# The second batch's gathers moved behind the last quarter's modulation, and the third tile's maxima put ahead of the third quarter's combination

## The reference, cut to what matters

```
x  = x + gb * (w0 * y[expert0] + w1 * y[expert1])          # end of layer 0
h  = layernorm(x) * (1 + ca) + sa                          # 'modulation'
B  = (h W_qk) W_anchor^T * scale      # 16 heads x 64 anchors = 1024 logits a token
attn = softmax(B) over the 64 anchors of each head
s    = sum over tokens of attn
out  = attn ((attn^T v) / s)
x  = x + ga * (out W_out + b_out)
h  = layernorm(x) * (1 + cb) + sb
x  = x + gb * ffn(h)                                       # gated, three more layers
```

## Time and profile before

| | us |
|---|---|
| median of 3 runs | 779.26 (777.74 to 782.41) |
| the profiled execution | 780.26, span 778.5 |
| TensorE busy | 654.1 (84%) |
| VectorE busy | 570.3 (73%) |
| ScalarE busy | 400.4 (51%) |
| GpSimd busy | 277.6 (36%) |
| batch 0's attention up to its last sum | from about 301 to 363 |
| the same stage of batch 1 | up to 477 |
| mean granted TensorE clock | 0.926 |

### The profile page before, as it was taken

How to read it: one execution, slowest core, us unless ns; L and a number is a source line. 1 busy time by engine, 2 the same in 40 slices (tenths; PEclk the granted TensorE clock), 3 DMA queues, 4 the chain that set the end, 5 groups by cost and what they waited for, 6 DMA issues and landing times.

```text
span 778.5 us, 9648 instructions
## 1 busy us (share of the span) xinstructions
PE 654.1 (84%) x2985; PEld 470.0 (60%) x2985; DVE 570.3 (73%) x1441; ACT 400.4 (51%) x698; POOL 277.6 (36%) x229
## 2 busy tenths in 40 slices
PE   5777550399999995879989899899899899899897
PEld 2666540388878883446468555478555478556575
DVE  4889959279866736996976786866796866783763
ACT  3646233277777732334375444485443585442573
POOL 6457778200000026686202375211485120341100
PEclk9979755699999985989999999999999999999999
DMA  6441587778898610001000000000100000000000
GB/s 212 136 177 52 202 296 275 233 250 267 250 304 307 215 58 27 18 21 28 0 1 0 35 28 21 1 0 1 41 23 20 0 1 1 27 1 1 0 1 28
DMA packets 25779, 69.26 MB, mean 89 GB/s; under 512 B 5296, under 2 KB 8384, under 8 KB 24384
## 3 DMA queue, kind: packets, MB, share of 16 engines
q1 hardware_dynamic: 21632, 60.24, 23.0%
q0 software_dynamic: 4096, 8.40, 3.6%
HBM read 46.46 MB, written 22.16 MB: 88 GB/s over the span
## 4 chain that ended last, share of the span: by engine, by line
PE 58%; DVE 21%; POOL 7%; issue 6%; DMA 4%; ACT 4%; SPq 1%; DVEq 0%; ACTq 0%; POOLq 0%
PE ps L1685 14%; PE ps L1687 8%; PE ps L1681 8%; PE ps L1942 6%; PE ps L1689 6%; PE ps L1688 6%; DVE stats L1061 3%; POOL rows_by_expert L605 3%; PE ps L1960 2%; PE ps L1930 2%; DMA wbuf<-w_split 2%; DVE ring L1565 2%; DMA raw<-in_w 1%; DVE yb L1465 1%; DVE cmat L1641 1%
## 5 line engine op out<-in xcount | busy, mean ns | idle before, releaser
L652 POOL DMA_INDIRECT yb<-y_by_expert,ypos x64 | 63.3, 989 | 158.2 <-DMA y_by_expert<-ysb 142.6
L1685 PE MATMUL ps<-hid,fh 128*128 128x512 f32 x256 | 103.5, 404 | 5.1 <-DVE hid L1549 5.1
L1687 PE MATMUL ps<-hid,fh 128*128 128x512 f32 x256 | 101.4, 396 | 0.0
L605 POOL DMA_INDIRECT rows_by_expert<-h,pos x64 | 71.1, 1112 | 25.0 <-issue 18.9
L700 POOL TENSOR_TENSOR misc<-misc,ring 128x1024 f32<-128x1024 f32 x28 | 66.0, 2357 | 33.8 <-DVE ring L1539 28.7
L1549 DVE TENSOR_TENSOR hid<-ring,hid 128x512 fp32r<-128x512 f32 x56 | 38.6, 689 | 41.7 <-ACT hid L941 40.1
L1942 PE MATMUL ps<-ring,hn 128*128 128x512 f32 x112 | 56.5, 628 | 5.3 <-DVE ring L1539 5.3
L1685 PEld LDWEIGHTS ps<-hid,fh 128*128 128x128 f32 x256 | 48.2, 188 | 21.0 <-DVE hid L1549 10.3
L1960 PE MATMUL ps<-attnT,cmat 128*128 128x512 f32 x128 | 56.9, 592 | 0.0
L1687 PEld LDWEIGHTS ps<-hid,fh 128*128 128x128 f32 x256 | 48.3, 188 | 10.7
L998 ACT ACTIVATE ring<-ps 128x1024 f32<-128x1024 f32 x32 | 32.8, 1025 | 42.6 <-PE ps L1930 42.4
(11 more groups left out here) (326 smaller groups left out, 1702.4 us busy)
## 6 DMA issues: line engine op xcount, KB each, us to landing
wbuf<-w_split SPq DMA_DIRECT2D x46, 512.0 KB, 5.6
w_split<-parts SPq DMA_DIRECT2D x4, 2048.0 KB, 7.7
raw<-in_w SPq DMA_DIRECT2D x8, 512.0 KB, 8.5
xs<-rows_by_expert SPq DMA_DIRECT2D x16, 256.0 KB, 5.4
y_by_expert<-ysb SPq DMA_DIRECT2D x16, 256.0 KB, 4.5
ffn_raw<-in_ffn SPq DMA_DIRECT2D x1, 2816.0 KB, 11.1
rows_by_expert<-zeros SPq DMA_DIRECT2D x9, 256.0 KB, 2.5
xa<-in_x SPq DMA_DIRECT2D x4, 512.0 KB, 4.9
```

Of the source, the lines that this page charges most:

```text
L605: gp.indirect_dma_start(disp, bass.IndirectOffsetOnAxis(pos[:, b, k, t:t + 1].bitcast(U32), 0), h1[:, b % 2, t, :], None).then_inc(scatter ...
L652: gp.indirect_dma_start(yb[:, k, t, :], None, ydisp, bass.IndirectOffsetOnAxis(ypos[:, b, k, t:t + 1].bitcast(U32), 0))\
L1685: te.matmul(out_, w(0), x(0), start=first, stop=False)
L1687: return te.matmul(out_, w(0), x(1), start=False, stop=last_)
```

## The change

GpSimd's list in batch 0 loses the two gathers ahead of the first addition and those behind the additions of tiles 1 and 2. Three gathers now stand behind each of the additions of tiles 3 to 7, and the last one behind them; all 16 are still issued in batch 0. Later batches are as before. In VectorE's list `neg_max(2, 0)` comes ahead of `combine(0, 2)`.

```diff
                 if b == 0:
                     gather(0, places[14:16])
                     prepared(2, 0)
-                if more:
+                if b and more:
                     gather(b + 1, places[0:2])
                 for t in range(1, T):
                     pool.wait_ge(*dve_attn.now(t, b))
...
                     if b == 0 and t == 2:
                         modulate(3, 0)
-                    if more and t < T - 2:
+                    if b == 0 and t > 2:
+
+                        gather(1, places[3 * (t - 3):3 * (t - 2)])
+                    if b and more and t < T - 2:
                         gather(b + 1, places[2 * t:2 * t + 2])
                 if more:
-                    gather(b + 1, places[2 * (T - 2):])
+                    gather(b + 1, places[2 * (T - 2) if b else 3 * (T - 3):])
...
                 sums(0, b)
-                if b == 0:
-                    combine(0, 2)
                 if b:
                     residual("F", 1, ffn_bank(1, "y"), b - 1)
                 neg_max(2, b)
                 if b == 0:
+                    combine(0, 2)
                     normalized("L1a", 2, 0)
```

## The result

| | before | changed |
|---|---|---|
| median of 5 runs | 778.51 us (776.27 to 782.41) | 782.98 us (781.77 to 783.75) |
| ratio to before | | 1.0053, 95% interval 1.0027 to 1.0079 |
| profiled execution | 780.26, span 778.5 | 783.75, span 782.0 |
| mean granted clock | 0.926 | 0.927 |

The change made the kernel 4.5 us slower by the medians, 2.1 to 6.2 us by the interval. The forecast was 784.0, the range 778.0 to 788.0.

The account below looks back on a forecast made before the run. The chain of waits was taken to run through GpSimd's second addition and fourth-quarter modulation, then TensorE. Profiled 780.3 + 3.8 (late last sum) + 0.9 (clock) = 785.0 us, so median 784.0; range 778.0 to 788.0.

Parts of the forecast that it names:

- the two terms: First attention's end: TensorE's wait for GpSimd's last sum, +3.8 us, and its clock falling behind that wait, +0.9 us.
- rival (d): TensorE's clock falls long at 367, or again in the 6.2 us cycles: +7 to +8, 786.8 us; chance 0.15.
- Step 1: VectorE, third tile's maxima ahead of the third quarter's combination: root wait of 0.84 us exposed, second scaling about 1.0 us later.
- Steps 2 and 3: GpSimd's first two additions without gathers ahead: VectorE's fourth and fifth maxima casts held, third addition at 338.0 instead of 340.7.
- Step 4: Three gathers per tile on GpSimd: cycle 6.2 us, seventh addition at 364.65 instead of 360.50, TensorE's small matmuls +3.8 us.
- Rival (a): Gathers beside VectorE's scaling not stretched: cycle about 6.0, last sum 2.0 to 2.8 late, 781.7 us; chance 0.20.
- Step 5: TensorE's clock falls behind the wait for the last sum: +0.9 us after 0.85 slack, bounds 0 and +4.
- Rival (c): TensorE's gap at 329.7 closes, clock stays up, modulation earlier, attention ends 2.0 us earlier: 777.3 us; chance 0.08.

Follow-up runs that it names:

- e1: Kernel before with only the third tile's maxima moved ahead of the third quarter's combination, gathers as before; stage 73.01 us against 71.93, ratio 0.9983.
- e11: e6 with three gathers ahead of the fourth quarter's root and two between it and the second addition; stage 70.45 us, no ratio given.
- e8: Kernel before with three of its last four gathers moved between the sixth and seventh additions; stage 78.19 us, ratio 1.0067.
- e3: Changed kernel without gathers between the sixth and seventh additions, seven behind the last; stage 72.56 us, ratio 1.0027.
- e9: Kernel before with two of its last four gathers moved between the sixth and seventh additions; stage 76.99 us, ratio 1.0054.
- e10: e6 with VectorE's list of the kernel before; stage 68.12 us, no ratio given.
- e12: The kernel of e10 on a second occasion, timed against the kernel before; stage 68.12 us, ratio 0.9971.
- e6: Changed kernel with four gathers ahead of the fourth quarter's root, two behind additions of tiles 3 to 5, six behind the last; stage 68.66 us, ratio 0.9959.
- e5: e3 with one gather moved between the fourth quarter's root and the second addition; stage 72.70 us, no ratio given.
- e7: e6 with one more gather between the fourth quarter's root and the second addition, five behind the last; stage 70.48 us, ratio 0.9961.
- e2: Changed kernel with VectorE's old list, so only the gathers moved; stage 78.06 us, ratio 1.0052.
- e4: Changed kernel with three surplus 512-column matmuls on TensorE ahead of its first-batch wait for the last sum; stage 76.64 us, ratio 1.0028.

## Why the prediction was right

The path was the forecast one: the gathers make the last sum late, TensorE waits for it, and its clock falls behind the wait. The size was in part luck: +4.7 us forecast, +4.5 measured by the medians, with an interval of 2.1 to 6.2. By the stage, which repeats better, the two terms were off in opposite directions: 3.1 for the late last sum instead of 3.8, and 3.2 for the clock instead of 0.9, together 6.3 (6.36 at the outputs, 0.1 of it given back behind them). That lies between the forecast and rival (d), which had +7 to +8 for a long fall of the clock.

- **Step 1** said the second tile's scaling 1.0 later and the root's wait 0.84 exposed. Measured: 0.84, and the scaling ended 1.1 later (319.20 + 1.24 from t0, 9.81, against 320.73 + 1.26, 8.75). e1 confirmed +1.08 for the stage when this is done alone.
- **Steps 2 and 3** said additions at 323.1 and 332.0, casts held 1.2 and 2.0, the gap of TensorE 3.6, the third addition 338.0. On before's scale (+2.61) they came at 323.12 and 331.92, 1.28 and 1.96, 3.34, and 337.79. e11 showed that freeing the held cast with gathers brings nothing. The prediction did not say why the third addition comes earlier; the rows above do: the scaling of 3.27 us is back at 1.25.
- **Step 4** said the third gather is stretched and the cycles 7.1, 6.4 and 6.3, then 6.85; measured 7.06, 6.12, 6.11 and 6.80. The stretch was 0.1 us in the steady cycles. The step itself worked out a cycle of 6.2 and then wrote 6.4 and 6.3 without a reason; it was 0.7 us late by the sixth addition. e8 proved the last link by itself, e3 its reverse.
- **Rival (a)**: that the gathers are not stretched beside a scaling is refuted by 1.91, 1.76 and 1.08 us for gathers that start inside one. Its cycle of 6.0 was still nearer to the measured 6.12 than the forecast's 6.4, since the stretch is small where the scaling is nearly over. The inference of the Trainium skill that the prediction cites ("SBUF — State Buffer", section "Who interferes with whom"), by which a gather and a two-input scaling don't meet, does not hold for these gathers. Their rows name `ypos` as an input besides; whether what waits is the reading of it or the writing of the descriptors, no run separates.
- **Step 5** named the fall of the clock and mis-sized it. It lasted 6 us of full work, not 3, and the slack of 0.85 that I set against it was no cover: the slow products feed VectorE's `cmat` matrices, so VectorE's combinations behind them came 6.3 us later, as late as TensorE. I had misread: they show the end of four transposes and VectorE's next addition to x, which it reaches without idling; that interval is still 0.76 us in the changed kernel. The small matmuls took 1.7 us more, the products and what hangs on them 1.5. I had this as the upper bound (+4) and in rival (d), and should have taken what lay nearest, the fall at 332.5. Read rightly, that row also gives the size: a mean of 0.67 over 9.8 us, the rest at 1.0, is 6.5 us at half clock, an estimate of 3.2 us lost and not 4.
- **When the clock falls** could not be worked out from a few rows of one execution. It fell behind the last sum as forecast. But it also fell behind 1.60 us in e9, and did not fall behind 2.03 (e1), 2.02 (e9) and 3.38 us (e10, e12) of other waits, so the length of the wait alone does not decide it.
- **Rival (c)**, the aim of the change, was real only in part: the modulation and the third addition do come earlier, and e6 turns that into 3.3 us, once the gathers go where GpSimd idles anyway.

## What to carry to other kernels

Work that is moved off one critical wait must be followed to where it lands: look for the next instruction on that queue which somebody waits for with no slack. Here the seventh addition had 0.3 us, and three gathers in front of it cost ten times that. Put such work where the queue already idles (5.8 us ahead of the root), not evenly behind it. And expect that a wait of TensorE ahead of critical products can cost more than its length: behind 1.6 and 2.85 us of waiting for the last sum the clock took another 3.2 to 3.4. Look at the clock behind the same wait in more than one execution before you put a small difference down to the order of the work.

## What the runs showed of the hardware

- From the start of the one-column matmuls to the outputs it took 5.24 or 5.25 us in all nine executions in which they had no wait ahead (before, e1, e3, e5, e6, e7, e10, e11, e12). Where TensorE had waited for the last sum, 1.60 us (e9), 2.84 (changed) and 2.85 (e2, e8), the clock fell to 0.5 and it took 8.68, 8.48, 8.46 and 8.66 us: 3.2 to 3.4 more, whatever the length of the wait.
- The clock also fell where TensorE had been idle for only 0.27 us just before (e4), in the products behind the one-column matmuls.
- Elsewhere the same wait was followed by a fall or by none. For the fifth tile's maxima: 2.01 (before) and 1.99 us (e8) with a fall, 2.02 (e9) and 2.03 (e1) with none; 3.34 (changed, e2, e3, e4) and 3.37 (e6) with a fall, 3.38 (e10, e12) with none. What else decides it no run shows.
- VectorE's small instruction between the maxima and the transpose was held to the end of GpSimd's addition when it started 0.64 us (subtraction, 3.03 us in e5), 0.66 us (3.05 us in e7) or 0.38 us (the 2.77 us cast of the earlier trace rows) ahead of the addition's recorded start, beside the gather directly ahead of it. Beside such a gather but 0.75 us ahead it was free (0.17 us at 323.45 in the kernel before), and so was the one of e11, with another gather in between. What GpSimd holds in that time the profile doesn't show.
